# Layer 0 of a two-layer residual kernel: one block-diagonal 128x128 product, or two 64-row products

## The reference

```python
# layer 0: each batch picks one of 8 subjects (itok_B_0_7)
x = x + einsum('bct,bcd->bdt', x, weights[subject]) + bias[subject][:, :, None]
# layer 1: each batch picks one of 8 adapters (itok_B_0_6)
H     = einsum('btd,od->bto', x, W)                    # W is 512x512
delta = (x @ A[adapter].T) @ Bm[adapter].T * scal[adapter]   # rank 16
x = x + H + delta
```

## Time and profile before

| what | value |
|---|---|
| median of 3 runs | 275.24 us (274.54 to 275.3) |
| span of the profiled execution | 271.8 us, 6814 instructions |
| that execution's own time | the three runs above are the times on record; the median lies 3.4 us over the span |
| mean granted TensorE clock | 0.997 of full speed (its column shows 1.00 from the start) |
| HBM read and written | 19.67 MB and 16.78 MB, 134 GB/s over the span |
| mean busy share of the DMA engines by slices of the span | 0.1 to 0.6 |

### The profile page before, as it was taken

How to read it: one execution, slowest core, us unless ns; L and a number is a source line. 1 busy time by engine, 2 the same in 40 slices (tenths; PEclk the granted TensorE clock), 3 DMA queues, 4 the chain that set the end, 5 groups by cost and what they waited for, 6 DMA issues and landing times.

```text
span 271.8 us, 6814 instructions
## 1 busy us (share of the span) xinstructions
PE 256.0 (94%) x1393; PEld 220.1 (81%) x1394; DVE 148.6 (55%) x244; ACT 113.3 (42%) x189; POOL 87.9 (32%) x285
## 2 busy tenths in 40 slices
PE   0598999999999999999999999999999999999993
PEld 0476888888888888888888888888888888888882
DVE  5668677555655556555665566555655553344300
ACT  2254554433544354433444353443434433323511
POOL 7355223433333332333432342333332333330000
PEclk9999999999999999999999999999999999999998
DMA  6662554454554545444554455543655455455221
GB/s 122 160 164 59 158 145 144 129 148 123 168 137 134 153 135 154 136 134 133 170 141 129 141 144 154 146 128 114 171 147 143 131 152 156 138 144 148 63 55 39
DMA packets 25821, 36.62 MB, mean 135 GB/s; under 512 B 6736, under 2 KB 8784, under 8 KB 25808
## 3 DMA queue, kind: packets, MB, share of 16 engines
q1 hardware_dynamic: 20400, 28.06, 37.1%
q10 hardware_dynamic: 5408, 8.40, 11.9%
HBM read 19.67 MB, written 16.78 MB: 134 GB/s over the span
## 4 chain that ended last, share of the span: by engine, by line
PE 91%; DVE 3%; DMA 3%; ACT 1%; issue 1%; SPq 0%; ACTq 0%; DVEq 0%
PE ps L696 66%; PE ps L682 21%; PE ps L671 3%; DMA a_f<-in_L_cond_A_dram 2%; DMA ids_i<-in_itok_B_dram 1%; PE ps L653 1%; DVE x_lo L494 1%; DVE m_lo L481 1%; PE ps L643 0%; ACT x_hi L559 0%; DVE prec_n L382 0%; DVE a_parts L460 0%; DVE m_f L475 0%; ACT m_hi L553 0%; ACT a_parts L542 0%
## 5 line engine op out<-in xcount | busy, mean ns | idle before, releaser
L696 PE MATMUL ps<-m_hi,x_hi 128*128 x264 | 108.6, 411 | 0.8 <-DVE x_lo L494 0.4
L696 PE MATMUL ps<-m_lo,x_hi 128*128 x264 | 103.1, 390 | 0.0
L696 PE MATMUL ps<-m_hi,x_lo 128*128 x264 | 103.1, 390 | 0.0
L353 POOL COPY p_pair<-p_all 64x64 f32 x128 | 52.0, 406 | 149.8 <-issue 73.3
L682 PEld LDWEIGHTS ps<-p_pair,x_ring 128*128 128x128 f32 x512 | 67.5, 193 | 5.4 <-DMA x_ring<-in_x_dram 0.4
L494 DVE TENSOR_TENSOR x_lo<-x,x_hi 128x512 fp32r<-128x512 f32 x64 | 44.5, 695 | 47.1 <-ACT x_hi L559 47.1
L682 PE MATMUL ps<-p_pair,x_ring 128*128 128x128 f32 x512 | 68.1, 276 | 0.0
L568 ACT ACTIVATE o_ring<-ps 128x512 f32<-128x512 f32 x60 | 35.8, 596 | 74.2 <-PE ps L696 74.0
L487 DVE TENSOR_TENSOR x<-ps,bias_pair 128x512 f32<-128x512 f32 x64 | 44.2, 691 | 35.9 <-PE ps L682 35.2
L559 ACT ACTIVATE x_hi<-x 128x512 fp32r<-128x512 f32 x64 | 40.5, 632 | 43.3 <-DVE x L487 43.3
L696 PEld LDWEIGHTS ps<-m_hi,x_lo 128*128 128x128 f32 x264 | 49.6, 188 | 10.6
(11 more groups left out here) (82 smaller groups left out, 54.5 us busy)
## 6 DMA issues: line engine op xcount, KB each, us to landing
x_ring<-in_x_dram SPq DMA_DIRECT2D x128, 128.0 KB, 2.6
out_dram<-o_ring SPq DMA_DIRECT2D x64, 128.0 KB, 2.6
out_dram<-o_ring ACTq DMA_DIRECT2D x64, 128.0 KB, 2.3
o_ring<-in_L_cond_W_dram SPq DMA_DIRECT2D x4, 256.0 KB, 4.4
a_f<-in_L_cond_A_dram SPq DMA_DIRECT2D x8, 128.0 KB
b_nat<-in_L_cond_Bm_dram SPq DMA_DIRECT2D x1, 256.0 KB, 4.0
p_all<-in_L_cond_weights_dram SPq DMA_DIRECT2D x2, 128.0 KB, 4.2
bias_all<-in_fside_8xS_dram SPq DMA_DIRECT2D x1, 256.0 KB, 4.7
```

Source lines behind the costliest of these rows:

```text
L353: nc.gpsimd.tensor_copy(p_pair[rows, slot, rows], p_all[rows, ds(s[half], 1), :] .rearrange("p s d -> p (s d)")).then_inc(pair_ready, 1)
L696: mm = nc.tensor.matmul(ps[:, bank, :], part[:, u % 2, c, :], m[:, ds(k * (TC * T) + c * T, T)], start=(c == 0 and part is x1_hi and m is ...
```

## The change

Layer 0's product of a chunk becomes two, one for each batch of the pair: 64 partitions of x by the 64x64 weight of that batch, in the upper and the lower half of the partitions. The first writes one PSUM bank and the second the next one. `p_pair` shrinks to 64 columns and needs no zeros, so its memset goes. The banks of layer 0 become 0 and 1 for even pairs, 6 and 7 for odd ones; the transposed Bm moves from bank 6 to bank 4, and `turn_b` waits for `m_added` in place of `b_ready`. `x1_add` reads both banks in one instruction. The semaphore counts of `consts` fall by one.

```diff
-        p_pair = sb("p_pair", [P, XR, P])
+        p_pair = sb("p_pair", [P, XR, C])
...
-        b_turned_at = ps[:, 6, :].rearrange("p (c n) -> p n c", c=TC)
+        b_turned_at = ps[:, 4, :].rearrange("p (c n) -> p n c", c=TC)
+
+        def l0_banks(u):
+
+            return 6 * (u % 2)
...
-            nc.gpsimd.memset(p_pair[:], 0.0).then_inc(consts, 1)
-            pool.wait_ge(consts, 5)
+            pool.wait_ge(consts, 4)
...
-                    nc.gpsimd.tensor_copy(p_pair[rows, slot, rows], p_all[rows, ds(s[half], 1), :]
+                    nc.gpsimd.tensor_copy(p_pair[rows, slot, :], p_all[rows, ds(s[half], 1), :]
                                           .rearrange("p s d -> p (s d)")).then_inc(pair_ready, 1)
...
-                nc.vector.tensor_tensor(x1[:, u % 2], ps[:, u % 2, :].rearrange("p (c n) -> p c n", c=TC),
-                                        bias_pair[:, u % XR, :].unsqueeze(1).to_broadcast([P, TC, P]),
-                                        ALU.add).then_inc(x1_ready, 1)
+                bank = l0_banks(u)
+                nc.vector.tensor_tensor(x1[:, u % 2].rearrange("p c (h d) -> p c h d", h=2),
+                                        ps[:, bank:bank + 2, 0:TC * C].rearrange("p h (c d) -> p c h d", c=TC),
+                                        bias_pair[:, u % XR, :].rearrange("p (h d) -> p h d", h=2).unsqueeze(1)
+                                        .to_broadcast([P, TC, 2, C]), ALU.add).then_inc(x1_ready, 1)
...
-                at_least(pe, b_ready, i)
+                at_least(pe, m_added, i * TC - 1)
                 for c in range(TC):
-                    mm = nc.tensor.transpose(ps[:, 6, c * P:c * P + P],
+                    mm = nc.tensor.transpose(ps[:, 4, c * P:c * P + P],
                                              b_dup[:, c].rearrange("p g r -> p (g r)"), ident[:])
...
                 at_least(pe, x1_ready, j - 1)
+                bank = l0_banks(u)
                 for c in range(TC):
-                    mm = nc.tensor.matmul(ps[:, u % 2, c * P:c * P + P], x_ring[:, slot, c * P:c * P + P],
-                                          p_pair[:, slot, :], start=True, stop=True)
+                    for half in range(2):
+                        rows = slice(C * half, C * half + C)
+                        mm = nc.tensor.matmul(ps[:, bank + half, c * C:c * C + C], x_ring[rows, slot, c * P:c * P + P],
+                                              p_pair[rows, slot, :], start=True, stop=True)
                 mm.then_inc(l0_done, 1)
```

More of the change, by code:

```diff
@@ L296, in _ @@
             nc.gpsimd.memset(neg[:], 0.0).then_inc(consts, 1)
-            pool.wait_ge(consts, 8)
+            pool.wait_ge(consts, 7)
             nc.gpsimd.affine_select(out=neg[:, 0:1], in_=neg[:, 0:1], compare_op=ALU.is_gt, fill=-1.0,
@@ L302, in _ @@
                                     base=R, pattern=[[0, 1]], channel_multiplier=-1).then_inc(consts, 1)
-            pool.wait_ge(consts, 10)
+            pool.wait_ge(consts, 9)
             nc.gpsimd.affine_select(out=neg[:, 1:2], in_=neg[:, 1:2], compare_op=ALU.is_gt, fill=0.0,
                                     base=2 * R, pattern=[[0, 1]], channel_multiplier=-1).then_inc(consts, 1)
-            pool.wait_ge(consts, 11)
+            pool.wait_ge(consts, 10)
             nc.gpsimd.affine_select(out=neg[:, 1:2], in_=neg[:, 1:2], compare_op=ALU.is_gt, fill=-1.0,
@@ L310, in _ @@
             nc.gpsimd.memset(b_dup[:], 0.0).then_inc(consts, 1)
+            pool.wait_ge(consts, 12)
+            nc.gpsimd.memset(a_parts[GR:P, :].bitcast(F32), 0.0).then_inc(consts, 1)
             pool.wait_ge(consts, 13)
-            nc.gpsimd.memset(a_parts[GR:P, :].bitcast(F32), 0.0).then_inc(consts, 1)
-            pool.wait_ge(consts, 14)
             pool.wait_ge(bnat_in, 16)
@@ L388, in _ @@
             iota_done = did(nc.vector.tensor_copy(iota[:], iota_i[:]))
-            dve.wait_ge(consts, 7)
+            dve.wait_ge(consts, 6)
             nc.vector.tensor_copy(ones_b[:], ones[:]).then_inc(consts_b, 1)
@@ L495, in x1_split @@
                                         ALU.subtract).then_inc(x1_lo_ready, 1)
-            dve.wait_ge(consts, 14)
+            dve.wait_ge(consts, 13)
             b_split(0)
```

## The result

The changed kernel takes 298.81 us (median of 4 runs, 298.43 to 299.26) against 275.27 us before: 23.5 us more, a ratio of 1.089 with a 95% interval of 1.085 to 1.094. Slower, as forecast, but by little more than a third of the 64 us of the forecast.

The account below looks back on a forecast made before the run. TensorE was taken to bound the kernel; layer 0's loads in turn (+54.4 us from pair 3 on, +0.9 and +0.7 at the start) and switches (+8.1) gave 275.2 + 64.1 = 339.3 us, range 274 to 352.

Parts of the forecast that it names:

- What bounds the kernel: TensorE, 91% of the chain; layer 0's 0.89 us a pair is on it, so a slower layer 0 pays in full.
- parts 4 to 6: x1_add reading two banks, turn_b's wait for m_added, and the memset of p_pair gone: 0 us each.
- The loads as the pace of layer 0: On TensorE, a 128-column weight load takes about 107 to 111 ns, as much as layer 0's whole spacing.
- Part 1: Layer 0's weight loads go from 8 to 16 a pair, taken in turn: +0.89 us a pair.
- the upper bound: Layer 0's 16 loads each cost 111 ns in turn: 1.78 us a pair, +0.89.
- rival A: Layer 0's halves load beside each other; 283 us, or 275 with free switches; chance 0.18 with switches.
- the lower bound: Layer 0's two halves load beside each other, 111 ns a couple: 0.89 us a pair as before.
- D: Rival: the change does nothing on TensorE, two loads at once and no switch cost; 275 us, chance 0.07.
- Part 3: Changing between 128-row and 64-row work twice per pair on TensorE: 2 x 0.063 x 64 = 8.1 us, ends 0 to 31.
- My price for it (13 us): TensorE drains at each switch between tiling modes: 2 x 0.10 x 64 = 13 us, the sum then 344 us.
- the 3.4 us that I carried: The median of runs, 275.24 us, lies 3.4 us above the profiled span of 271.8; added to the forecast span.
- C: Rival: the load path does not bind, layer 0 falls towards 0.43 us; 246 us, 254 with switches; chance 0.13.

Follow-up runs that it names:

- all_rows: Changed kernel with each of layer 0's 16 products a pair over all 128 rows, block-diagonal operand and memset back: 329.3 us.
- one_row_group: Changed kernel with the second half's products also read from partitions 0 to 63: 357.3 us.
- before_by_twos: Kernel before the change with layer 0 issued for two pairs in a row at every second step: 275.03 us.
- experiment 6: Changed kernel with only the first two pairs' layer 0 as 16 products of all 128 rows: 299.4 us, the change beside it 297.9.
- experiment 7: Changed kernel, each 64-row product split into two of 64 stationary columns, small product ahead: 272.4 us; with two pairs in a row 269.6 us.
- half_by_half: Changed kernel with layer 0's loops swapped, four products of the upper half of the partitions first, then four of the lower: 332.1 us.
- experiments 4 and 5: Changed kernel with layer 0 for two pairs in a row, 288.5 us; with one small product more ahead of layer 0, 301.8, or in its middle, 317.1.

## Why the prediction was wrong

**What bounds the kernel** held. TensorE's share is unchanged (94%), the chain from the first layer 0 to the last layer 1 lies on it alone, and x1_add (0.69 us), turn_b's new wait and the missing memset cost nothing, as parts 4 to 6 said.

**The loads as the pace of layer 0** held, too. all_rows shows 108 ns per load with half the columns behind it.

**Part 1 is the step that failed.** It took the upper bound, each of 16 loads in turn, +0.89 us a pair, since in the trace loads were "never two at once". But all loads of that trace were of 128 rows, and such rows can't tell what two 64-row loads do; that was said there as a weakness of rival A's evidence and not given its weight. The value was the lower bound: 0 for the loads, measured as rounds of two loads every 0.112 us, the pace of one load before. all_rows and one_row_group show where the upper bound would have been right (329 and 357 us). The Trainium skill's page "TensorEngine Tiling (Array Packing)", Key Properties, has the rule (different tiles load and multiply in parallel), to which I had given a chance of 0.18 (0.25 with D): the trace agrees. That the kernel got slower was forecast mostly for a reason that did not hold: 56 of the 64 us were loads, and the borders, 8.1 us in the sum, are what made it slower. To that extent the right direction was luck.

**Part 3 was mis-sized, by a factor of almost three.** I took 2 x 0.063 us a pair. Measured: 0.15 on the way in and 0.21 on the way out, together 0.36. The reading was at fault. The rows said more than I took from them: the load of L653 starts at 10.44, 0.07 us before the end of L661's last matmul (10.51). In the changed kernel the load at 153.39 comes 0.07 before the end of layer 1's last matmul (153.07 + 0.39 = 153.46), and the one at 154.43 comes 0.07 before layer 0's end (154.50). So a load across the border waits until the last matmul is nearly through; nothing of L653's delay need be put down to the semaphore, which I had subtracted, and what was left missed what a border costs in full: most of the way through the array, plus a load that nothing hides. From rows of the kernel before: out, the load starts 0.27 - 0.07 = 0.20 us after the start of layer 0's last matmul instead of at once, hidden in no part; in, it starts 0.39 - 0.07 = 0.32 after layer 1's last, whose stream of 0.23 hides part, and the rest is 0.09 plus the first half of a load. The Trainium skill's rule of a drain at each change of mode (the same page and section) fits this: the next load waits for the last matmul. My price for it (13 us) was short for the same reason.

**The sum that would have been right**: 0 for loads and 64 x 0.35 = 22 us for borders, 298 us. That is rival A with the right price; I had it at 283. Of the profiled span's +25.3 us, 21.5 come after the fourth layer 0 starts (at 32.65 us, before at 28.85), which is 61 x 0.35 = 21.4; the other 3.8 lie in the start. The first layer 0 starts 0.8 later, after a wait for x (17.09 against 16.27; in before_by_twos at 17.23, so this moves without the change), three pairs of borders are 1.1, and the 1.9 left are put down to the low clock, whose cause is open (experiment 6). The median rose by 23.5 and the span by 25.3, since the 3.4 us that I carried from span to median was not a constant: in every later run, the change's too, the time is 1.7 us over its span, so the profiled execution of the kernel before was probably about 1.7 us faster than its median. (By its own terms the forecast's range ends at 331 and 362, not 332 and 363.)

**C**, the faster case, was wrong for this change: with two row groups the load path still binds at 0.112 us a round. Its thought, that layer 0 could fall towards 0.45 us, came true only in experiment 7, by cutting the stationary columns of a load.

## What to carry to other kernels

When a trace holds only one shape, it can bound what another shape does, but not choose between the bounds; the nearest row then deserves no more weight than the other bound, and a run with one thing changed (as all_rows and one_row_group here) settles it. Before splitting a product into tiles, ask what each tile path carries: here the loads set the pace, and splitting the rows alone doubled the loads at two a time, a gain of nothing, and 0.36 us lost for two borders. Split in the direction that shortens the bound (64 stationary columns halve each load, four at once), and keep the tiled work in one long stretch, as the borders are paid per stretch.

## What the runs showed of the hardware

- A plain float32 load costs two cycles of 2.4 GHz a column, with 64 rows as with 128: loads of 128 columns last 188 and 192 ns and follow each other after 0.112 us, loads of 64 columns last 135 ns. Two 64x128 tiles load at once (a round of two every 0.112 us), and four 64x64 tiles (a round of four every 0.058 us); 64 such loads with their matmuls take 1.09 us. Loads of one row group run in turn (one_row_group, 1.93 us against 1.04).
- The border between 128-row and 64-row work costs 0.15 us in and 0.21 us out at the full clock; the next load starts 0.07 us before the recorded end of the last matmul, in all 61 pairs. With a small bf16 product between, two borders cost 0.24.
- TensorE starts a product in another row group while an earlier one of the first row group is still to come (half_by_half, eight matmuls started in 0.39 us in the middle of a layer 0, as read there): products of different row groups don't keep the program's order of starts.
- A label of the profile such as "0.35 <-POOL p_pair L356" can name the last semaphore where the time is a border's. The copies that a layer 0 waits for had ended 9 us or more before, from the fourth pair on, and experiments 4 and 5 moved the gap without touching them.
